# Graph layer kernel, first stage: which queue writes the first sixteen blocks of zeros of the aggregate table, and when

## The reference

```
ni, nj = x[src], x[tgt]
mask   = (edge_attr[:, 0:1] < 8)
f      = elu(concat([ni, nj, ni - nj, edge_attr[:, :65]]) @ Wf + bf) * mask
a      = tanh((ni @ Wq) * (f @ Wk) * scale @ Wa)
a_sum  = segment_sum(a, src)
z      = exp(a) / exp(a_sum)[src] * f
aggr   = segment_sum(z, src)
x      = layernorm(x + (x + aggr) @ Wu + bu)
```

## Time and profile before

| | us |
|---|---|
| median of 3 runs | 4009.34 |
| lowest and highest | 4005.22, 4010.04 |
| profiled execution, its time | 4005.84 |
| profiled execution, span of the trace | 4003.9 |

### The profile page before, as it was taken

How to read it: one execution, slowest core, us unless ns; L and a number is a source line. 1 busy time by engine, 2 the same in 40 slices (tenths; PEclk the granted TensorE clock), 3 DMA queues, 4 the chain that set the end, 5 groups by cost and what they waited for, 6 DMA issues and landing times.

```text
span 4003.9 us, 25580 instructions
## 1 busy us (share of the span) xinstructions
PE 865.0 (22%) x5636; PEld 736.9 (18%) x5636; DVE 2286.9 (57%) x5661; ACT 1211.9 (30%) x2640; POOL 2966.9 (74%) x2952
## 2 busy tenths in 40 slices
PE   4746777765777000000000000000000000000000
PEld 3745565664555000000000000000000000000000
DVE  6867555553998016555466665666656666633333
ACT  1213666741787001111122221222221222133333
POOL 5778877776777777777677776777767777677776
PEclk8877988987999555555555555555555555555555
DMA  8543333333887013333356665566654444455565
GB/s 270 135 64 63 74 67 62 63 67 72 251 259 236 8 12 106 106 106 106 107 200 211 211 211 188 199 210 210 210 196 141 158 158 158 160 142 156 157 161 139
DMA packets 311964, 581.62 MB, mean 145 GB/s; under 512 B 93856, under 2 KB 172246, under 8 KB 311810
## 3 DMA queue, kind: packets, MB, share of 16 engines
q1 hardware_dynamic: 192034, 394.81, 29.5%
q0 software_dynamic: 116576, 169.55, 19.4%
q10 hardware_dynamic: 3200, 15.63, 1.2%
HBM read 332.00 MB, written 247.75 MB: 145 GB/s over the span
## 4 chain that ended last, share of the span: by engine, by line
POOL 55%; issue 18%; DMA 1%; DVE 1%; ACT 0%; POOLq 0%; PE 0%; DVEq 0%; ACTq 0%
POOL gx L1124 36%; POOL edge_s L884 9%; POOL ag L1341 9%; DVE psum L1229 0%; DMA u<-cross,first_idx 0%; DMA gx<-u,far_row 0%; DVE us L1239 0%; DMA total<-cross_sum,first_idx 0%; DVE psum L1210 0%; DVE tn L1194 0%; DMA u<-us 0%; ACT psum L1175 0%; ACT normed L839 0%; DMA out_dram<-normed 0%; DMA gx<-x,far_i 0%
## 5 line engine op out<-in xcount | busy, mean ns | idle before, releaser
L1124 POOL DMA_INDIRECT gx<-u,far_row x1176 | 1109.7, 944 | 368.7 <-issue 357.5
L1210 DVE TENSOR_TENSOR psum<-gx,psum 128x1024 f32<-128x1024 f32 (+1 forms) x200 | 241.6, 1208 | 711.0 <-DMA gx<-u,far_row 505.0
L1175 ACT ACTIVATE psum<-us 128x512 f32<-128x512 f32 x288 | 173.1, 601 | 1186.0 <-DVE tn L1194 626.3
L884 POOL DMA_INDIRECT edge_s<-edge_d,edge_id x392 | 375.9, 959 | 133.3 <-issue 126.4
L1124 POOL DMA_INDIRECT gx<-x,far_i x392 | 373.4, 952 | 119.5 <-issue 119.5
L1341 POOL DMA_INDIRECT ag<-total,fin_idx x390 | 369.8, 948 | 122.4 <-issue 118.6
L1229 DVE TENSOR_TENSOR_SCAN psum<-goes_on,psum 128x1024 f32<-128x1024 f32 (+1 forms) x200 | 449.1, 2246 | 2.0
L1145 PE MATMUL psum<-last_z,chain 128*128 128x128 f32 x8 | 3.2, 501 | 2002.8 <-DVE last_z L1235 2002.8
L330 POOL DMA_INDIRECT agg<-summed,sc_idx x196 | 325.3, 1660 | 81.7 <-issue 57.2
L1145 PEld LDWEIGHTS psum<-last_z,chain 128*128 128x128 f32 x8 | 2.0, 310 | 2003.7 <-DVE last_z L1235 2003.7
L1163 ACT COPY goes_on<-cont_in 128x1024 f32<-128x1024 f32 (+1 forms) x200 | 202.8, 1015 | 394.7 <-DVE cont_in L1008 201.9
(11 more groups left out here) (173 smaller groups left out, 2974.8 us busy)
## 6 DMA issues: line engine op xcount, KB each, us to landing
u<-us SPq DMA_DIRECT2D x144, 512.0 KB, 3.1
total<-tn SPq DMA_DIRECT2D x144, 512.0 KB, 3.2
tp<-total SPq DMA_DIRECT2D x98, 512.0 KB, 5.3
ag<-agg SPq DMA_DIRECT2D x65, 396.0 KB
x<-normed SPq DMA_DIRECT2D x65, 387.0 KB, 2.9
xc<-x SPq DMA_DIRECT2D x65, 387.0 KB, 4.6
tp<-u SPq DMA_DIRECT2D x49, 512.0 KB, 5.2
xc<-in_x_dram SPq DMA_DIRECT2D x65, 384.0 KB
```

What stands on the lines that cost most here:

```text
L884: g.indirect_dma_start(edge_s[:, c, :], None, edge_d[:, :], bass.IndirectOffsetOnAxis(ap=edge_id[:, c:c + 1], axis=0)).then_inc(edge_in[c ...
L1124: g.indirect_dma_start(gx[b % 4][:, j * width:(j + 1) * width], None, source[:, :], bass.IndirectOffsetOnAxis(ap=idx[:, c:c + 1], axis=0)) ...
L1210: return v.tensor_tensor(zf.rearrange("p (h f) j -> p j h f", h=H), by_head(gxv(b % 4)[:, c0:c1, 0:D]), per_head(wt[:, b * B + c0:b * B + ...
```

## The change

ACT no longer issues sixteen blocks before its step 0. It issues three in each of seven steps (ACT_STEPS = 7, so 21 blocks, the last behind `exp_att` of s = 6), and SP issues SP0 = 16 blocks at s = 2, then three at each of s = 3 to 6 (28 blocks). An instruction that loads ACT's function table stands at the start of its stream. The whole diff:

```
-ACT0, SP0 = 16, 8
-ACT_STEPS = 4
-ACT_BLOCKS = ACT0 + 3 * ACT_STEPS
+ACT_STEPS = 7
+ACT_BLOCKS = 3 * ACT_STEPS
+SP0 = 16
...
             def _(act):
+                act.preload_act_table_set("exp_and_others")
                 act.wait_ge(zero_set, 1)
...
-                for n in range(ACT0):
-                    clear(n)
...
                     if s < ACT_STEPS:
-                        clear(ACT0 + s * 3)
+                        clear(s * 3)
...
-                        clear(ACT0 + s * 3 + 1)
+                        clear(s * 3 + 1)
...
-                        clear(ACT0 + s * 3 + 2)
+                        clear(s * 3 + 2)
```

## The result

| | before | after |
|---|---|---|
| median of 6 runs, us | 4008.63 | 4026.82 |
| lowest and highest | 4005.22, 4010.79 | 4022.82, 4028.13 |
| profiled execution: time, span | 4005.84, 4003.9 | 4026.29, 4024.4 |

The ratio after to before is 1.0044, 95% interval 1.0034 to 1.0055: the change makes the kernel slower by 18.2 us in the medians, 20.5 us in the two spans.

What follows compares the result with a forecast made beforehand. POOL bounds the kernel, so its end moves with the first scatter: +16.4 us for the later last block plus 1.1 lost at step 3 make +17.5, on a median of 4009.34: 4027 us, range 4013 to 4036.

Steps and rivals of the forecast that it cites:

- POOL's first scatter sets the end: From 141.24 us POOL issues indirect DMAs back to back, so the program's end moves as much as its first scatter.
- Step 0: Start of the stage: copies 10.5, table load 1.3 and late gather 4.8 us go away; `neg` 16.6 us earlier, at 35.9.
- The gain is spent at step 3: DVE waits for loads behind SP's sixteen blocks; they land at 93 us (86 to 97), 1.1 us later than before.
- the seven blocks of ACT: ACT's blocks from steps 0 to 2, 12.1 us of DMA work counted before step 3's loads land; called the softest term.
- the 2.9 us: In the count to step 3's loads: blocks behind the loads served early on some engines, kept from the old row.
- The second way, by issues: Step 3's landing from SP's issue times, about 2.45 us a block: `attr` issued at 74.6, landing at about 94.7.
- The rule on turns: DMA engines alternate between queue rows, so ACT is served in full and SP's queue pays for all seven blocks; landing stays 93.
- rival 1: At step 3, SP's queue gets more of the engines, loads land at 81; first scatter +5.5 us, 4015; chance 0.13.
- The last block: ACT's third of s = 6, behind `exp_att`, lands at 157.6 in before's time, moving the first scatter by +16.4 us.
- rival 4: Backlog lasts: loads at 97, 3 us more in each of two steps; first scatter +27.5 us, 4037; chance 0.08.
- Steps 4 to 6: ACT's nine new blocks slide some 4 us of DMA work back; slack covers it: 0, with a bound of 3 us.
- rival 2: No stall at step 3: the 16.6 us gain reaches step 6 whole, scatter at 141.0, 4009, no change; chance 0.10.

Runs made afterwards that it cites:

- the burst alone: Kernel before, with ACT issuing 8 blocks instead of 16 ahead of its step 0 and SP 16 instead of 8 at s = 2: 4017.61 us, ratio 1.0024.

## Why the prediction was right, and where it was not

**POOL's first scatter sets the end: right.** The table above is the evidence. The cost of 20.5 us in the span is the 24.9 us of the scatter less 4.5 us by which the rest of this execution happened to be shorter; between the kernels that difference varies by 7.6.

**Step 0: right.** `neg` at 36.11 against 35.9 forecast. The terms did not all come as written: the copies started 17.7 us earlier (16.6 in the sum), with PE's first transpose at 24.66, 5.9 us earlier instead of 4.8, and the weight matmuls ahead of `neg` gave 1.2 us back, being longer at the slower pace (6.90 us from the first of them to `neg`, 5.67 before).

**The gain is spent at step 3: right in mechanism, the size missed.** I gave the landing of the loads as 93, between ends of 86 and 97; `same` started at 99.9, outside my ends, and the same burst put it at 100.7 and 101.4 in two other kernels, so this is not scatter. The price of a block did not fail, nor did the seven blocks of ACT. The DMA queues of the changed kernel from 45.1 us (the first landing as forecast) to 99.2 show the sum's terms one by one (packets, MB, share of the 16 engines):

```profile
q1 hardware_dynamic: 3025, 9.97, 59.3%
q10 hardware_dynamic: 774, 3.85, 23.7%
q0 software_dynamic: 856, 1.75, 8.7%
```

Of these 54.1 us ACT's queue had 12.8 (12.1 in the sum), SP's 32.1 (30.2: its blocks, the loads and the 2.9 kept for blocks behind them), the gathers 4.7 (4.1), and for 4.4 us the engines were idle (0). The sum's 46.4 us were thus 7.7 too few, and the mis-sized term is the 2.9 us for unequal progress of the engines, carried over from a row of eight blocks: SP's queue had 4.8 us beyond its fifteen blocks and the loads, and idle engines, put at nothing, took 4.4 more. The view by windows shows when they were idle:

```profile
60.00:80.00 20.00, 8.39 (x62) 8.19 (x61) 14.04 (x48) 1.69 (x5) 12.97 (x13) 0.76 0.99 312
80.00:100.00 20.00, 0.68 (x4) 0.68 (x5) 0.31 (x2) 0.00 (x0) 0.00 (x0) 0.50 0.78 242
```

In the last 20 us before the loads landed the engines were busy for only 78% (second number from the end), with everybody waiting. Without ACT's blocks they were busy for 97% up to the landing (44.2 to 78.8 us). Of the sixteen arrivals of `attr` five came at 81.1 to 81.4, ten at 89.7 to 94.8 and the last at 99.2. Two other kernels with the burst of sixteen beside many blocks of ACT show the same (ACT's blocks ending at step 4: five at 81.4 to 81.6, the last at 100.0; the burst alone: 81.1 to 81.5, and 100.7). Their mean, 89.1 us, is near what a count of work gives; the consumer waits for the last. Why the shares drift apart so far with both queues deep no run here tells; it stays open.

The second way, by issues, used a row in which ACT's blocks were already in the price. It was nearer (94.7, by its own terms 94.9), and missed at two places: a block behind the first two held SP for 2.60 us and not 2.45, and the wait from issue to landing had grown from 17.9 to 20.3 us for `key_row`.

**The rule on turns.** The row, before, had both queues in work at once, and in the runs SP's row paid for ACT's blocks, 15.1 us in the mean for nine, so rival 1, by which it would not, has nothing left. The Trainium skill (DMA: Bandwidth & Descriptors, Queues, rings and completion order) says that each DMA engine takes turns between the queue rows that have work. The shares of the queues agree with that; no view here shows single turns.

**The last block: right.** The wait of 16.43 us was forecast at some 16. The scatter started 5.1 us after the block's issue (5.3 taken). In the scatter's own sum, 16.4 and 1.1, the first term came out at 157.3 - 141.2 = 16.1 and the second at 8.8, the lateness of `exp_att` of step 6 (161.12 against 152.29). Taking ACT's last blocks away gave 10.0 us back; of the 14.9 left, 13.0 are POOL's own later arrival and 2.0 a wait for a block. The whole shift of the scatter, 24.9 us, lies outside the forecast's +11 to +23; it came near rival 4's +27.5, but with all of the lateness made at step 3 and none in the steps 4 to 6, where rival 4 put 6 us. The rows that I forecast from step 3 on came late by as much: `same` at 99.9 for 92 to 94, ACT's last block at 161.1 for about 153, the scatter at 166.2 for 157 to 160.

**Steps 4 to 6: right.** From step 3 to `exp_att` of step 6 the lateness went from 8.0 to 8.8 us; I had 0 with a bound of 3.

**The number.** 4027 against 4026.82 is luck in its last digits: the term of step 3 was 6.9 us too small, the rest of the profiled execution was 4.5 us shorter, which no run explains, and that of before lay further under its median (2.8 us) than that of the changed kernel (0.5). The medians moved by 18.2 us, the forecast 17.5.

**What I did not see:** that the idle DMA time ahead of 39 us (busy for 41% from 14 to 39 us) is a loss of its own. I took it as a point for rival 2, not as capacity given away. The three kernels that repair one or both of my two costs and leave it idle (busy for 35 to 40% from 20 to 40 us) stay slower than before (1.0018, 1.0035 and 1.0012), and all three that fill it from SP (98 to 100%) are faster (0.9978 to 0.9985). It is not the only loss: the burst alone kept 81% there and was still slower (1.0024), by its stall at step 3.

## What to carry to other kernels

When a bulk transfer is moved off a queue that holds up compute, look at what the DMA engines do in the time that it leaves: if they go idle and are full later, the transfer has to be issued in that same time by an engine with nothing to do, ahead of its next wait. A burst in front of a load on one queue is a wait for the consumer of that load. Counting the work of all queues in front of it gave the mean arrival of the load's shares here; the consumer waits for the last share, which came 5 to 10 us behind the mean with both queues deep and 3 to 5 us with few or no blocks on ACT's, so that distance needs a term of its own. And for the last transfer that a barrier needs, read when its issuing engine gets there in the old trace, since an edit that gains early can lose it all at that one wait.

## What the runs showed of the hardware that was not expected

- A load behind a burst arrives in shares that drift apart. Behind SP's sixteen blocks the sixteen arrivals of `attr` spread over 6.8 us with no block of ACT beside them (71.9 to 78.7), over 4.8 with three and over 18.1 with nine (81.1 to 99.2), while each of ACT's blocks moved their mean by 1.7 us.
- With both queues deep, one small load's issue held SP for 8.52 us (`key_row` at 79.56), where the same load took 2.45 us in the kernel before. With the same burst in two other kernels it was 7.04 and 8.09, and 2.70 with nothing on ACT.
- In the changed kernel PE made its weight matmuls of step 0 at a pair every 0.43 us until 35.3 us and then at about twice that pace, at a granted clock of 1.00 all through from 29 to 36.5 us (the two levels are 1.2 and 2.4 GHz); the granted clock of a stretch did not tell the pace there.
